# A four-layer block on one Trainium2 core: the later part of a woven feed-forward placed one head later, and the context copies of the next batch placed in other heads

## The chip, the core and the metric

The kernel runs on one core of one Trainium2 chip. The metric is the device time of one execution in microseconds (us), the median of several. The kernel before takes 576.02 us (median of three runs, 575.34 to 576.35).

## The reference

Four residual steps act on `x` (4 batches, 256 tokens, 256 columns): a selective state-space scan over a context, a mixture of 64 experts (8 per token), a cross-attention with 16 heads, and a feed-forward with weights rounded to -1, 0, 1. Each is added under a tanh gate. Only the last two matter here.

```python
x = x + tanh(g_xattn[0]) * L0_xattn(ctx_1024, layernorm(x), ...)
x = x + tanh(g_ffn[0])   * L0_ffn(layernorm(x), ...)          # experts
x = x + tanh(g_xattn[1]) * L1_xattn(layernorm(x), ctx_1024, ...)
x = x + tanh(g_ffn[1])   * L1_ffn(x, ...)

# L1_xattn, per batch and head (16 heads, 8 key/value heads, width 128)
scores = q @ k.T / sqrt(128); attn = softmax(scores); out = attn @ v; return out @ Wo
# L1_ffn
h = silu(bitlinear158(x, w1, b1))     # rms norm, 8-bit rounding of rows, ternary weights
h = gelu(h)
h = layer_norm(h, ln_g, ln_b)
return bitlinear158(h, w2, b2)        # inner width 1024
```

## The kernel before, in words

Every engine has its own program, written in the order in which it shall run, and waits on counting semaphores. Scan, routing and experts come first. From about 283 us on, the attention of the four batches runs head by head, in 64 turns called slots here: slot s is head s mod 16 of batch s div 16. Key and query weights are folded into one matrix `mqk` per head, value and output weights into `nvo`, so that the keys are the context itself. Products of fp32 accuracy are made of three products of rounded parts: a value is copied as fp32r (`..._high`, on ACT), and its remainder is made beside it (`..._low`, on DVE).

In one slot each engine does this for heads of different age:

- PE turns the weights of head s-3 (`turn_p`, L1617), makes the scores of head s (`cT,qT`, L1567 to L1569), the values of head s-4 (L1628), the query product of head s+2 (`xnT,mqk`) and the output product of head s-5 (`nvo,oT`).
- ACT copies the turned weights of head s-3 (`pT`, L1027), the value product of head s-4 (`oT`, L1033) and the query of head s+2 (`qT`, L1012), and makes the exponentials of head s (`pr`, L1019).
- DVE makes the reciprocal of head s-1 (`pinv`, L2293), masks the scores of head s (L2284), and makes the remainders `oT` and `qT` (L2254).
- POOL normalises head s-1 (`pn`, L688). It waits for the reciprocal; PE's turn and ACT's next exponentials but one wait for it.

Into this the feed-forward of the batch before is woven, for the first three batches. `feeds(slot)` returns for a slot the pairs (f, at): batch f, and `at` = slot - 16 (f + 1), from 0 to 27. The tables in each engine's loop say what a batch does at which `at`. Batches 0 and 1 (f < B - 2) share one table, batch 2 has another. For batches 0 and 1 the back part, from the gelu on, is: `gelu` (13), `rest_rows` (14), `middle`, `deviations` (15, 16), `variance`, `centred` (16), `root_of` with `frt` (POOL, L696), `normal_hidden` (17), `squares`, `largest`, `mean_square` (17, 18), `root_of` with `frm`, `scaled` and `scale_round` (19), `turn_hidden` (20), `turned_hidden`, `out_of` and `finish` (22). The front part of the next batch begins at its own `at` 5, which is `at` 21 of this one: `front_stats` 5, `front_norm` 6, `front_round` 7, `turn_in` 8, `into` 9 and 11. `hidden`, `silu` and `gated` follow at 10 to 13.

Two more things stand between the heads. The next batch's inputs of attention: its context as fp32r (`context_high`, ACT, L993, tile `cT`), the remainder of that (`context_low`, DVE), the context rows (`context_rows`, ACT, L997, tile `cS`), the normalised rows (`norm3`, `turn_xn3`, `norm_high`, `norm_low`, tile `xnT`, in heads 12 and 13). And POOL's `gather` (L672): 16 indirect DMAs fetch the expert rows of batch b + 1 in heads 0 to 7 of batch b, for b = 0, 1, 2. Batch 3 has none.

Of the kernel before, what the change touches and what calls it, by code (L numbers as in the profile page):

```python
# [60 lines left out]
def build_program(nc, t, out):  # L61

    with ExitStack() as ctx:
# [491 lines left out]
        def _(pool):  # L555
# [171 lines left out]
            for slot in range(NH * B + 5):  # L727
# [29 lines left out]
                for f, at in feeds(slot):  # L757
                    if at == 5:
                        root_front(f)
                    if at == (14 if f < B - 2 else 12):  # L760
                        rest_rows(f)
                    if at == (15 if f < B - 2 else 14):
                        root_of(f, 1, 0)
                    if at == (17 if f < B - 2 else 19):
                        root_of(f, 1, 1)
# [10 lines left out]
        def _(act):  # L776
# [344 lines left out]
            for slot in range(NH * B + 5):  # L1121
# [3 lines left out]
                if b + 1 < B:  # L1125
                    if h == 13:
                        context_high(b + 1)
                for f, at in feeds(slot):
                    if at == 9 and f < B - 2:
                        turned(f)  # L1130
                    if at == (12 if f < B - 2 else 10):
                        silu(f, 1)
                    if at == 12 and f == B - 2:
                        gelu(f, 0)
                        gelu(f, 1)
                    if at == 18 and f < B - 2:
                        squares(f, 1)
                    if at == 22 and f < B - 2:
                        turned_hidden(f, 0)
                    if at == (22 if f < B - 2 else 20):  # L1140
                        turned_hidden(f, 1)
# [4 lines left out]
                for f, at in feeds(slot):  # L1146
                    if at == 8 and f == B - 2:
                        turned(f)
                    if at == 13 and f == B - 2:
                        deviations(f, 0)  # L1150
                    if at == 16 and f < B - 2:
                        deviations(f, 1)
                    if at == 16 and f == B - 2:
                        squares(f, 1)
                    if at == 19 and f == B - 2:
                        turned_hidden(f, 0)
# [9 lines left out]
                for f, at in feeds(slot):  # L1166
                    if at == (11 if f < B - 2 else 9):
                        silu(f, 0)
                    if at == 13 and f < B - 2:
                        gelu(f, 0)  # L1170
                        gelu(f, 1)
                    if at == 15 and f < B - 2:
                        deviations(f, 0)
                    if at == 14 and f == B - 2:
                        deviations(f, 1)
                    if at == (17 if f < B - 2 else 15):
                        squares(f, 0)
# [21 lines left out]
        def _(pe):  # L1199
# [536 lines left out]
            for slot in range(NH * B + 9):  # L1736
# [17 lines left out]
                for f, at in feeds(slot):  # L1754
# [6 lines left out]
                    if at == (20 if f < B - 2 else 19):  # L1761
                        turn_hidden(f, 0)
                    if at == (20 if f < B - 2 else 24):
                        turn_hidden(f, 1)
                    if at == (22 if f < B - 2 else 24):
# [20 lines left out]
        def _(dve):  # L1786
# [836 lines left out]
            for slot in range(NH * B + 12):  # L2623
# [8 lines left out]
                if b + 1 < B:  # L2632
# [11 lines left out]
                    if h == 13:  # L2644
                        context_low(b + 1)
                for f, at in feeds(slot):
# [12 lines left out]
                    if at == (16 if f < B - 2 else 14):  # L2659
# [3 lines left out]
                    if at == (17 if f < B - 2 else 15):  # L2663
                        normal_hidden(f, 0)
                    if at == 17 and f < B - 2:
                        normal_hidden(f, 1)
                    if at == (18 if f < B - 2 else 16):
# [3 lines left out]
                    if at == 18 and f < B - 2:  # L2671
                        mean_square(f)
                    if at == (19 if f < B - 2 else 17):
# [19 lines left out]
                for f, at in feeds(slot):  # L2693
# [13 lines left out]
                    if at == (15 if f < B - 2 else 12):  # L2707
                        middle(f)
                    if at == 16 and f < B - 2:
# [4 lines left out]
                    if at == 18 and f < B - 2:  # L2714
# [3 lines left out]
                    if at == (19 if f < B - 2 else 17):  # L2718
                        scale_round(f, 0)
                    if at == 19 and f < B - 2:  # L2720
                        scale_round(f, 1)
                    if at == 22 and f < B - 2:
# [64 lines left out]
```

## Time and profile before

| | before |
|---|---|
| median of 3 runs | 576.02 us |
| profiled execution | 575.79 us |
| its span | 573.8 us |
| mean granted TensorE clock | 0.955 |
| attention, slots 0 to 63 | about 283 to 531 us |
| busy: PE, DVE, ACT, POOL | 84%, 82%, 64%, 49% |

The profile is of one execution, which took 575.79 us; its span from first to last instruction is 573.8 us, so 2.0 us lie around it, and it stands 0.23 us below the median. A matmul row of PE has a modelled end. An idle time in brackets stands before the instruction of its row, with what ended it.

### The profile page before, as it was taken

Reading aid. Unit: us, or ns where it says so; the run is one execution under the profiler, and the core shown is the slowest. Engines: PE = TensorE matmul, PEld = TensorE weight load, DVE = VectorE, ACT = ScalarE, POOL = GpSimd, SP = SyncE. Lnnn points to the kernel's source line nnn. Section 1 sums busy time; section 2 is a strip of 40 time slices with the busy share of each in tenths; the row PEclk is TensorE's granted clock in tenths of the full one; section 3 lists DMA queues with packets and bytes.
Section 4 is the critical chain, followed back from the end, with each engine's and each line's share of the span. In section 5 each row is a group of like instructions: output and inputs, shape, how many; then the busy total and the mean of one; then the engine's idle time right before and its main releaser. Section 6 shows DMA issues by size and latency. Waiting matters only on the chain.

```text
span 573.8 us, 10348 instructions
## 1 busy us (share of the span) xinstructions
PE 481.4 (84%) x3106; PEld 363.5 (63%) x3106; DVE 472.5 (82%) x1249; ACT 364.4 (64%) x831; POOL 279.7 (49%) x263
## 2 busy tenths in 40 slices
PE   6817777757889899999899999998699988998835
PEld 3302222222368766776888999987589888997714
DVE  4899999999997838788567857896899969875887
ACT  2785555435526555787676666679556796689544
POOL 4118777869520555630287368623874243333111
PEclk9956999999999999999899999999999999999876
DMA  5939400001045889893422012400335000000000
GB/s 155 228 84 324 125 0 1 1 1 37 1 136 154 272 256 295 233 306 104 167 58 63 1 38 57 56 2 1 53 57 61 0 2 2 19 2 1 0 20 19
DMA packets 45626, 48.63 MB, mean 85 GB/s; under 512 B 5660, under 2 KB 42118, under 8 KB 45574
## 3 DMA queue, kind: packets, MB, share of 16 engines
q1 hardware_dynamic: 41734, 36.46, 22.7%
q0 software_dynamic: 3840, 11.54, 9.1%
q8 instruction: 25, 0.41, 0.3%
q14 instruction: 27, 0.22, 0.1%
HBM read 41.43 MB, written 6.56 MB: 84 GB/s over the span
## 4 chain that ended last, share of the span: by engine, by line
PE 32%; DVE 23%; issue 22%; POOL 10%; ACT 7%; DMA 3%; SPq 1%; DVEq 1%; POOLq 0%; ACTq 0%
DVE hst L1884 7%; PE ps L1628 5%; PE ps L1567 3%; PE ps L1568 3%; PE ps L1569 3%; PE ps L1617 2%; POOL G L672 2%; POOL dbu L586 2%; POOL pn L688 2%; PE ps L1277 2%; PE ps L1485 2%; DVE hc L1893 2%; DMA G<-token_rows,idx_x 1%; POOL G L650 1%; PE ps L1521 1%
## 5 line engine op out<-in xcount | busy, mean ns | idle before, releaser
L688 POOL TENSOR_TENSOR pn<-pr,pinv 128x512 f32<-128x512 f32 x64 | 67.6, 1058 | 88.3 <-DVE pinv L2293 87.8
L586 POOL TENSOR_TENSOR dbu<-du,brow 128x512 f32<-128x512 f32 x64 | 81.3, 1282 | 41.6 <-DVE du L1877 23.1
L1277 PE MATMUL ps<-hc,ident 128*128 128x512 f32 x128 | 72.8, 657 | 27.2 <-DVE hc L1893 25.7
L1884 DVE TENSOR_TENSOR_SCAN hst<-ps,dbu 128x512 f32<-128x512 f32 x64 | 77.9, 1217 | 0.2 <-POOL dbu L586 0.2
L831 ACT ACTIVATE ps<-dtv,amat 128x510 f32<-128x510 f32 x64 | 44.1, 690 | 49.1 <-DVE hst L1884 48.2
L1019 ACT ACTIVATE pr<-ebuf,smin 128x256 f32<-128x256 f32 x128 | 63.7, 502 | 13.5 <-POOL pn L688 6.7
L1628 PE MATMUL ps<-pT,cS 128*128 128x256 f32 x256 | 66.5, 382 | 0.0
L1277 PEld LDWEIGHTS ps<-hc,ident 128*128 128x128 f32 x128 | 20.3, 195 | 66.9 <-DVE hc L1893 63.7
L650 POOL DMA_INDIRECT G<-token_rows,idx_x x32 | 37.7, 1179 | 44.2 <-DVE wkv L2019 20.8
L672 POOL DMA_INDIRECT G<-expert_out,idx_g x48 | 51.2, 1066 | 11.6 <-issue 10.7
L2284 DVE CUSTOM_DVE_ANT_0 ebuf<-ps,mbias 128x256 f32<-128x256 f32 x128 | 49.0, 420 | 5.9 <-issue 5.8
L1567 PE MATMUL ps<-xnT,mqk 128*128 128x256 f32 x128 | 46.9, 366 | 6.7 <-DVE qT L2254 3.5
L1617 PE MATMUL ps<-ident,pn 128*128 128x128 f32 x256 | 39.2, 276 | 9.0 <-POOL pn L688 5.1
L1628 PEld LDWEIGHTS ps<-pT,cS 128*128 128x128 f32 x256 | 44.3, 191 | 3.7
L1033 ACT ACTIVATE oT<-ps 128x256 fp32r<-128x256 f32 x64 | 24.4, 381 | 32.5 <-PE ps L1628 31.0
L1567 PE MATMUL ps<-cT,qT 128*128 128x256 f32 x128 | 41.8, 326 | 0.7 <-DVE smin L2284 0.6
L1893 DVE TENSOR_TENSOR hc<-hst,ps 128x512 f32<-128x512 f32 x64 | 42.3, 662 | 0.0
L1027 ACT ACTIVATE pT<-ps 128x512 f32<-128x512 f32 x64 | 37.3, 582 | 4.6 <-PE ps L1617 4.6
L1567 PE MATMUL ps<-nvo,oT 128*128 128x256 f32 x128 | 37.3, 292 | 2.5 <-DVE oT L2254 2.5
L2254 DVE TENSOR_TENSOR oT<-ps,oT 128x256 fp32r<-128x256 f32 x64 | 26.8, 419 | 14.0 <-ACT oT L1033 13.6
L1012 ACT ACTIVATE qT<-ps 128x256 fp32r<-128x256 f32 x64 | 24.6, 384 | 19.7 <-PE ps L1569 18.0
L1617 PEld LDWEIGHTS ps<-ident,pn 128*128 128x128 f32 x256 | 28.9, 141 | 12.6 <-POOL pn L688 6.5
(380 smaller groups left out, 1384.3 us busy)
## 6 DMA issues: line engine op xcount, KB each, us to landing
wdn<-in_L_ffn_wd SPq DMA_DIRECT2D x12, 384.0 KB
wgu<-in_L_ffn_wg SPq DMA_DIRECT2D x11, 384.0 KB
wgu<-in_L_ffn_wu SPq DMA_DIRECT2D x11, 384.0 KB
expert_out<-xn SPq DMA_DIRECT2D x11, 256.0 KB
wq<-in_L_xattn_Wq SPq DMA_DIRECT2D x2, 1024.0 KB, 9.3
wo<-in_L_xattn_Wo SPq DMA_DIRECT2D x1, 2048.0 KB, 15.8
wo<-in_L_ffn_w SPq DMA_DIRECT2D x2, 1024.0 KB, 7.0
expert_out<-pexp SPq DMA_DIRECT2D x5, 256.0 KB
```

The costliest lines, as they stand in the source:

```text
L586: nc.gpsimd.tensor_tensor(dbu[:, j, :], du[:, j % 2, 512 * hb:512 * hb + 512], brow[:, j // 2, :], ALU.mult).then_inc(pool_dbu, 1)
L672: nc.gpsimd.indirect_dma_start(G[:, cc, k, :], None, eout, bass.IndirectOffsetOnAxis(ap=idx_g[:, col:col + 1], axis=0), bounds_check=SLOTS ...
L688: nc.gpsimd.tensor_tensor(pn[:, h % 2], pr[:, h % 2], pinv[:, h % 2, :].unsqueeze(2).to_broadcast([P, 2, L]), ALU.mult)\
L831: A(bank(d).rearrange("p (b l) -> p b l", b=2)[:, :, 1:], dtv[:, d, 512 * hb:512 * hb + 512].rearrange("p (b l) -> p b l", b=2)[:, :, 1:], ...
L1019: last = A(pr[:, h % 2, tt, :], sneg[:, h % 2, tt, :], ACT.Exp, scale=-1.0, bias=smin[:, h % 2, tt:tt + 1], accum_out=psum_[:, h % 2, tt:t ...
L1277: pe.matmul(bank(2 + j % 2), ident[:], hc[:, j % 2, :], start=(isinstance(m, int) and m + k == 0), stop=(isinstance(m, int) and m + k == N ...
L1567: pe.matmul(o, lhs[0], rhs[0], start=start, stop=False)
L1617: last = pe.transpose(ps[:, 4, L * st + P * tt:L * st + P * tt + P], pn[:, h % 2, tt, P * st:P * st + P], ident[:])
L1628: last = pe.matmul(ps[:, 3 + 2 * (h % 2), 0:L], cS[:, b % 2, st, :], pT[:, h % 2, st, :], start=(st == 0), stop=(st == 1))
L1884: V.tensor_tensor_scan(hst[:, j, :], bank(j % 2), dbu[:, j, :], 0.0, ALU.mult, ALU.add)\
L1893: V.tensor_tensor(hc[:, j % 2, :], hst[:, j, :], bank(6 + j // 2), ALU.mult).then_inc(hc_ready, 1)
L2284: last = V.tensor_tensor_reduce(sneg[:, h % 2, tt, :], ps[:, 1, L * tt:L * tt + L], mbias[:, b, :], -(DH ** -0.5), 3e38, ALU.add, ALU.min, ...
```

## The change

The back part of batches 0 and 1 stands one slot later, from the gelu on, on all four engines: `at` 13 becomes 14, and so on up to 23 for `turned_hidden`, `out_of` and `finish`. Batch 2's table and all front parts stay. `context_high` of the next batch moves from head 13 to head 8, for three batches, and `context_low` from head 13 to head 14. No instruction is added or removed. SP's queue is the same.

```diff
--- before.py
+++ after.py
@@ -757,11 +757,11 @@
                 for f, at in feeds(slot):
                     if at == 5:
                         root_front(f)
-                    if at == (14 if f < B - 2 else 12):
+                    if at == (15 if f < B - 2 else 12):
                         rest_rows(f)
-                    if at == (15 if f < B - 2 else 14):
+                    if at == (16 if f < B - 2 else 14):
                         root_of(f, 1, 0)
-                    if at == (17 if f < B - 2 else 19):
+                    if at == (18 if f < B - 2 else 19):
                         root_of(f, 1, 1)
             tail_root_front(0)
             tail_root_front(1)
@@ -1123,7 +1123,7 @@
                 if 3 <= slot < NH * B + 3:
                     turned_p((slot - 3) // NH, (slot - 3) % NH)
                 if b + 1 < B:
-                    if h == 13:
+                    if h == 8:
                         context_high(b + 1)
                 for f, at in feeds(slot):
                     if at == 9 and f < B - 2:
@@ -1133,11 +1133,11 @@
                     if at == 12 and f == B - 2:
                         gelu(f, 0)
                         gelu(f, 1)
-                    if at == 18 and f < B - 2:
+                    if at == 19 and f < B - 2:
                         squares(f, 1)
-                    if at == 22 and f < B - 2:
+                    if at == 23 and f < B - 2:
                         turned_hidden(f, 0)
-                    if at == (22 if f < B - 2 else 20):
+                    if at == (23 if f < B - 2 else 20):
                         turned_hidden(f, 1)
                 if 4 <= slot < NH * B + 4:
                     o_high((slot - 4) // NH, (slot - 4) % NH)
@@ -1148,7 +1148,7 @@
                         turned(f)
                     if at == 13 and f == B - 2:
                         deviations(f, 0)
-                    if at == 16 and f < B - 2:
+                    if at == 17 and f < B - 2:
                         deviations(f, 1)
                     if at == 16 and f == B - 2:
                         squares(f, 1)
@@ -1166,14 +1166,14 @@
                 for f, at in feeds(slot):
                     if at == (11 if f < B - 2 else 9):
                         silu(f, 0)
-                    if at == 13 and f < B - 2:
+                    if at == 14 and f < B - 2:
                         gelu(f, 0)
                         gelu(f, 1)
-                    if at == 15 and f < B - 2:
+                    if at == 16 and f < B - 2:
                         deviations(f, 0)
                     if at == 14 and f == B - 2:
                         deviations(f, 1)
-                    if at == (17 if f < B - 2 else 15):
+                    if at == (18 if f < B - 2 else 15):
                         squares(f, 0)
             tail_turned(0)
             tail_tanh(0, 0)
@@ -1758,11 +1758,11 @@
                         into(f, 0)
                     if at == (11 if f < B - 2 else 9):
                         into(f, 1)
-                    if at == (20 if f < B - 2 else 19):
+                    if at == (21 if f < B - 2 else 19):
                         turn_hidden(f, 0)
-                    if at == (20 if f < B - 2 else 24):
+                    if at == (21 if f < B - 2 else 24):
                         turn_hidden(f, 1)
-                    if at == (22 if f < B - 2 else 24):
+                    if at == (23 if f < B - 2 else 24):
                         out_of(f)
             pe.wait_ge(s_masked, NH * B)
             keep_busy(1, 8)
@@ -2641,7 +2641,7 @@
                         add_experts(b + 1, 0)
                     if h == 12:
                         add_experts(b + 1, 1)
-                    if h == 13:
+                    if h == 14:
                         context_low(b + 1)
                 for f, at in feeds(slot):
                     if at == 5 and f < B - 2:
@@ -2656,21 +2656,21 @@
                         gated(f, 1)
                     if at == 15 and f == B - 2:
                         variance(f)
-                    if at == (16 if f < B - 2 else 14):
+                    if at == (17 if f < B - 2 else 14):
                         centred(f, 0)
                     if at == 15 and f == B - 2:
                         centred(f, 1)
-                    if at == (17 if f < B - 2 else 15):
+                    if at == (18 if f < B - 2 else 15):
                         normal_hidden(f, 0)
-                    if at == 17 and f < B - 2:
+                    if at == 18 and f < B - 2:
                         normal_hidden(f, 1)
-                    if at == (18 if f < B - 2 else 16):
+                    if at == (19 if f < B - 2 else 16):
                         largest(f, 0)
                     if at == 17 and f == B - 2:
                         largest(f, 1)
-                    if at == 18 and f < B - 2:
+                    if at == 19 and f < B - 2:
                         mean_square(f)
-                    if at == (19 if f < B - 2 else 17):
+                    if at == (20 if f < B - 2 else 17):
                         scaled(f)
                     if at == 19 and f == B - 2:
                         scale_round(f, 1)
@@ -2704,22 +2704,22 @@
                         hidden(f, 0)
                     if at == (11 if f < B - 2 else 9):
                         hidden(f, 1)
-                    if at == (15 if f < B - 2 else 12):
+                    if at == (16 if f < B - 2 else 12):
                         middle(f)
-                    if at == 16 and f < B - 2:
+                    if at == 17 and f < B - 2:
                         variance(f)
                         centred(f, 1)
                     if at == 15 and f == B - 2:
                         normal_hidden(f, 1)
-                    if at == 18 and f < B - 2:
+                    if at == 19 and f < B - 2:
                         largest(f, 1)
                     if at == 16 and f == B - 2:
                         mean_square(f)
-                    if at == (19 if f < B - 2 else 17):
+                    if at == (20 if f < B - 2 else 17):
                         scale_round(f, 0)
-                    if at == 19 and f < B - 2:
+                    if at == 20 and f < B - 2:
                         scale_round(f, 1)
-                    if at == 22 and f < B - 2:
+                    if at == 23 and f < B - 2:
                         finish(f)
             tail_add(0)
             tail_stats(0)
```

Three places show what it moves. ACT in heads 13 to 15 of batch 1, before (pT, oT, qT, pr are the copies and exponentials of the slots, xnT_0 the fp32r copy of the normalised rows, L1053 the gelu):

```order
L993 ACTIVATE cT<-ctxT 128x256
L1033 ACTIVATE oT<-ps 128x256
L1012 ACTIVATE qT<-ps 128x256
L1019 ACTIVATE pr,psum_<-ebuf,smin 128x256 x2
L1006 ACTIVATE xnT_0<-ps 128x512
L1053 ACT_TABLE_LOAD
L1053 ACTIVATE wgu,fsum<-wgu 128x1024 x2
L1027 ACTIVATE pT<-ps 128x512
L1033 ACTIVATE oT<-ps 128x256
L1012 ACTIVATE qT<-ps 128x256
L1019 ACT_TABLE_LOAD
```

and in the changed kernel, from the same oT copy on:

```order
L1033 ACTIVATE oT<-ps 128x256
L1012 ACTIVATE qT<-ps 128x256
L1019 ACTIVATE pr,psum_<-ebuf,smin 128x256 x2
L1006 ACTIVATE xnT_0<-ps 128x512
L1027 ACTIVATE pT<-ps 128x512
L1033 ACTIVATE oT<-ps 128x256
L1012 ACTIVATE qT<-ps 128x256
L1019 ACTIVATE pr,psum_<-ebuf,smin 128x256 x2
L997 ACTIVATE cS<-ctx_tm,alive 128x256
L1053 ACT_TABLE_LOAD
L1053 ACTIVATE wgu,fsum<-wgu 128x1024 x2
L1027 ACTIVATE pT<-ps 128x512
```

The gelus have moved behind one whole slot of copies and exponentials and behind the context rows; the context copy `cT` is gone from here.

POOL at the end of batch 1 and in heads 0 and 1 of batch 2 (`pn` is the normalising of a head, `frt` and `frm` the roots of the feed-forward, the `DMA` rows the gathers):

```order
-L688 TENSOR_TENSOR pn<-pr,pinv 128x512
-L696 TENSOR_TENSOR frt<-fve,mhalf 128x2
 L688 TENSOR_TENSOR pn<-pr,pinv 128x512
 L670 TENSOR_TENSOR spare_pool<-mhalf 128x2
 L672 DMA G<-expert_out,idx_g 128x256 x3
+L696 TENSOR_TENSOR frt<-fve,mhalf 128x2
 L688 TENSOR_TENSOR pn<-pr,pinv 128x512
 L672 DMA G<-expert_out,idx_g 128x256 x2
-L696 TENSOR_TENSOR frm<-fms,mhalf 128x2
 L688 TENSOR_TENSOR pn<-pr,pinv 128x512
 L672 DMA G<-expert_out,idx_g 128x256
+L696 TENSOR_TENSOR frm<-fms,mhalf 128x2
```

The root `frt` stood ahead of the first three gathers and the normalising before them; it now stands behind them. `frm` has moved past one normalising and one gather.

DVE in heads 3 to 5 of batch 2 (L2442 and L2445 are `scale_round`, L2304 adds a batch's attention to `x`):

```order
 L2442 TENSOR_SCALAR wgu<-wgu,fqs 128x1024
 L2445 TENSOR_SCALAR wdn<-wgu 128x1024
-L2293 RECIPROCAL pinv<-psum_ 128x2
-L2205 MEMSET spare 128x1
-L2284 ISA ebuf,smin<-ps,mbias 128x256
-L2284 ISA smin 128x1
-L2284 ISA ebuf,smin<-ps,mbias 128x256
-L2284 ISA smin 128x1
-L2254 TENSOR_TENSOR oT<-ps,oT 128x256
-L2254 TENSOR_TENSOR qT<-ps,qT 128x256
 L2304 SCALAR_TENSOR_TENSOR x<-ps,tg,x 128x512
 L2293 RECIPROCAL pinv<-psum_ 128x2
```

A slot of attention work that stood between the rounding and the addition to `x` has gone from between them: they now follow each other.

## Rows read from the trace of the kernel before

**Rows 1.** Busy time, share of the span and instructions of each engine.

```profile
PE 481.4 (84%) x3106; PEld 363.5 (63%) x3106; DVE 472.5 (82%) x1249; ACT 364.4 (64%) x831; POOL 279.7 (49%) x263
```

**Rows 2.** Engines by stretch: slots 19 to 22, 28 to 39, 44 to 55.

```profile
core 0: us, PE busy (x) PEld busy (x) DVE busy (x) ACT busy (x) POOL busy (x), PEclk, DMA share, GB/s
344.71:358.41 13.70, 13.70 (x107) 13.27 (x106) 10.09 (x44) 9.34 (x31) 11.45 (x13) 1.00 0.29 59
377.54:432.49 54.95, 46.56 (x352) 42.56 (x349) 45.44 (x142) 39.39 (x104) 34.16 (x32) 1.00 0.20 32
448.19:498.64 50.45, 45.66 (x351) 42.62 (x350) 42.94 (x141) 39.34 (x104) 18.35 (x17) 1.00 0.02 6
```

**Rows 3.** Timeline of PE (start us, us, instruction, idle before); scores start slots 31, 32, 34, 35, 38.

```profile
388.14 0.39 PE L1567 MATMUL ps<-xnT,mqk 128*128 128x256 f32 x1 [1.20 <-DVE xnT L2254]
...
391.11 0.36 PE L1567 MATMUL ps<-cT,qT 128*128 128x256 f32 x1
...
394.94 0.36 PE L1567 MATMUL ps<-cT,qT 128*128 128x256 f32 x1
...
402.65 0.36 PE L1567 MATMUL ps<-cT,qT 128*128 128x256 f32 x1
...
409.17 0.66 PE L1617 MATMUL ps<-ident,pn 128*128 128x128 f32 x4 [2.32 <-POOL pn L688]
409.58 0.37 PE L1567 MATMUL ps<-cT,qT 128*128 128x256 f32 x1
...
423.87 0.37 PE L1567 MATMUL ps<-cT,qT 128*128 128x256 f32 x1
```

**Rows 4.** Timeline of DVE, slot 29 (head 13 of batch 1).

```profile
384.90 0.79 DVE L2254 TENSOR_TENSOR cT<-ctxT,cT 128x256 fp32r<-128x256 f32 x1
385.61 1.21 DVE L2395 SCALAR_TENSOR_TENSOR wgu<-ebuf,wgu 128x1024 f32<-128x1024 f32 x1
...
387.41 0.68 DVE L2254 TENSOR_TENSOR xnT<-ps,xnT 128x512 fp32r<-128x512 f32 x1
```

**Rows 5.** Timeline of ACT, slots 29 and 30.

```profile
386.61 1.28 ACT L1053 ACT_TABLE_LOAD   x1
...
390.00 0.57 ACT L1027 ACTIVATE pT<-ps 128x512 f32<-128x512 f32 x1
...
391.14 1.28 ACT L1019 ACT_TABLE_LOAD   x1
```

**Rows 6.** Timeline of POOL, slots 31 to 33.

```profile
399.50 1.67 POOL L696 TENSOR_TENSOR frt<-fve,mhalf 128x2 f32<-128x2 f32 x1 [4.65 <-DVE fve L2406]
...
403.48 1.96 POOL L672 DMA_INDIRECT G<-expert_out,idx_g  x1 [0.16 <-issue]
...
408.07 1.05 POOL L688 TENSOR_TENSOR pn<-pr,pinv 128x512 f32<-128x512 f32 x1
```

**Rows 7.** Timeline of DVE, slots 33 and 35.

```profile
401.29 3.17 DVE L2418 SCALAR_TENSOR_TENSOR wgu<-wgu,frt 128x1024 f32<-128x1024 f32 x2
...
412.41 1.00 DVE L2337 TENSOR_TENSOR famax<-famax,frm 128x2 f32<-128x2 f32 x1 [0.80 <-POOL frm L696]
```

**Rows 8.** Timeline of DVE, slots 49 to 53, the same work a batch later.

```profile
471.76 3.95 DVE L2418 SCALAR_TENSOR_TENSOR wgu<-wgu,frt 128x1024 f32<-128x1024 f32 x2
...
480.83 0.51 DVE L2337 TENSOR_TENSOR famax<-famax,frm 128x2 f32<-128x2 f32 x1
...
482.84 0.74 DVE L2442 TENSOR_SCALAR wgu<-wgu,fqs 128x1024 f32<-128x1024 f32 x1
...
485.62 0.16 DVE L2293 RECIPROCAL pinv<-psum_ 128x2 f32<-128x2 f32 x1
...
487.06 0.74 DVE L2304 SCALAR_TENSOR_TENSOR x<-ps,tg,x 128x512 f32<-128x512 f32 x1
```

**Rows 9.** Timeline of PE, the scores of slots 54 and 57.

```profile
490.03 0.37 PE L1567 MATMUL ps<-cT,qT 128*128 128x256 f32 x1
...
502.31 0.37 PE L1567 MATMUL ps<-cT,qT 128*128 128x256 f32 x1
```

## The prediction

> **What bounds the kernel now.** I read the busy line first. PE is busy 84% of the span, DVE 82%, and ACT and POOL have room [rows 1], so neither PE nor DVE can be left alone. I then read the engines by stretch. In slots 19 to 22, with nothing woven in, PE is busy 13.70 of 13.70 us, 3.43 per slot, at full clock; DVE has 10.09 and ACT 9.34 (2.34 per slot) [rows 2]. So an untouched slot is PE's. The two stretches that the change reorders, slots 28 to 39 and 44 to 55, take 54.95 and 50.45 us, with PE busy for 46.56 and 45.66 [rows 2]: 8.4 and 4.8 us of gaps. All that the change can win at once lies there, and nothing in it makes PE's own work shorter. The timeline of PE says what ends the gaps: the remainder of the normalised rows (1.20 us, DVE) and a normalised head that is late (2.32 us, POOL) [rows 3]. So the question is at what time each slot's scores start, before and after. I walk the changed order by hand, with durations of rows of before, on the clock of the old trace; times after are estimates from these.
>
> **First stretch, step 1: heads 13 and 14.** The remainder of `cT` leaves slot 29 and reappears in slot 30. The next DVE instruction starts 0.71 us behind it [rows 4], so the remainder `xnT` starts at 386.70 in place of 387.41 [rows 4]; PE's wait of 1.20 becomes 0.49. In slot 30 the `pT` copy waited until 390.00 behind the table load at 386.61 and both gelus [rows 5]. It now starts at 386.6. So the scores of slot 31 start at about 389.3, not 391.11 [rows 3]: 1.8 us won.
>
> **Step 2: the gelus, a slot later.** The block is not shorter: 3.39 us from its table load to the next copy, plus 1.28 for loading the exponential's table back [rows 5], 4.67 us, where ACT has 3.43 - 2.34 = 1.09 to spare per slot. It now follows the copies, exponentials and context rows of slot 30: query copy at 388.45 (PE's queries end at 388.3), 0.3; exponentials 1.0; context rows 0.4; so 390.15. Plus 3.39 is 393.55; the next `pT` copy takes 0.57 (its row) [rows 5], so PE turns at 394.3 and scores at 394.65, against 394.94 [rows 3]. Of the 1.8 us, 1.5 are given back. **Won so far 0.3.** The exponentials of slot 31 come at 396.0, head 31's reciprocal at 397.1.
>
> **Step 3: POOL.** This is where I look for the gain. Before, `frt` waited 4.65 us for the variance and held back the normalising of head 31 until 401.15; then came three gathers, and head 32 was normalised only from 408.07 to 409.12 [rows 6], which is what PE waited 2.32 us for [rows 3]. Now `frt` stands behind the gathers. Head 31 is normalised at 397.3, the gathers run from 398.6 to 402.6 (about 1.3 each; they are 4 us in which POOL had waited for nothing useful), the variance is ready at 402.6, since the deviations are a slot later too, and `frt` takes 1.67 [rows 6], to 404.5 with its start. Head 32 is done at 405.5 and the scores of slot 35 start at 406.0, against 409.58 [rows 3]. **Won 3.6.** The two gathers of slot 33 now precede the normalising of head 33, done at 409.5, in time.
>
> **Step 4: DVE, slots 34 to 37.** It is the bound from here. Normals from 404.65, 3.1 us for the pair (3.17 in one trace stretch, 3.95 in the other) [rows 7, 8]; remainders of slot 34, 0.67; one masked head 0.77; `largest` twice and remainders, 3.1; mask of slot 36: the scales start at 413.0, against 412.41 one slot earlier [rows 7]. The scales with two remainders took 2.01 in the later batch (480.83 to 482.84) [rows 8], so 1.34 alone; in this batch the first tiny instruction alone took 1.00, not 0.51 [rows 7, 8], and the block ran to 3.4. I take 2.5. Remainders 0.67; the rounding 2.78 (482.84 to 485.62) [rows 8], or 3.0 beside gathers: 419.1. Before, a plain slot of 1.44 us (485.62 to 487.06) [rows 8] followed and let PE run on. Now the addition to `x` (0.66 of its 0.74) [rows 8] and the mask follow at once, and the scores of slot 38 start at 420.65, against 423.87 [rows 3]. **Won 3.2.**
>
> **Step 5: the front part of the next batch.** `finish` now stands in the slot of `front_round`, ahead of it, and needs the output product, which is behind all of PE's slot 39. DVE idles some 1.5 us, finishes (0.9) and rounds (2.1) until 432.5. That is just in time for PE; I charge 0.5 us for the stats one slot after the rounding. **First stretch: 2.7 us won.**
>
> **Second stretch.** Batch 3 has no gathers, so step 3 is absent: head 48 is normalised in step with `frt` before and after. Steps 1 and 2 win 0.3 again. The pair of normals is the slower one, 3.95 [rows 8], and PE waits for the query remainder behind it. Walked the same way, the scales start at 483.9, three microseconds after 480.83 [rows 8], of which a plain slot is only 1.44. Rounding ends at 488.7, the addition and the mask at 490.5, and the scores of slot 54 start at 490.6, against 490.03 [rows 9]: 0.6 lost. The stats, the norm and the late `finish` take 0.4 more: slot 57 at 503.3, against 502.31 [rows 9]. **1.0 us lost.**
>
> **The rest.** `context_high` (0.42 us) in heads 8 lies in ACT's 1.09 us of room; without that cover it would delay one value copy by 0.42. In batch 0 nothing else moves, and PE has no gap in heads 13 and 14 there. `rest_rows` a slot later hides in POOL's waiting. SP and the DMAs it issues are as before; POOL's gathers land earlier than they are used.
>
> **Sum.** -2.7 + 1.0 = -1.7 us. The profiled execution's 575.79 gives 574.1, the median 576.02 gives **574.3**. Bounds: the first stretch wins 0.3 if step 3 fails, and 4.7 if the scales take 1.34 (-1.2) and the late normals cost nothing more (-0.8). The second loses 1.6 if `finish` costs PE its whole 0.6 more, or wins 0.6 if PE keeps step 1. So 570.7 to 577.3.
>
> **A rule against the row.** The normals took 3.17 and 3.95 us for two [rows 7, 8], where a like operation with the same 1,024 columns took 1.21 [rows 4]; the long ones lie beside POOL's normalising and gathers, and one gather beside them took 1.96 [rows 6], others about 1.0. The Trainium skill, page "SBUF — State Buffer", section "Who interferes with whom", says that a VectorE instruction with two SBUF inputs contends with GpSimd's reads but, by inference, not with its descriptor generation. By that rule the gathers would leave the scales of step 4 alone.
>
> **Rivals.**
> - *Nothing held up by gathers.* The scales run in 1.34 us beside them, as in batch 3 [rows 8]. For it: that row. Against it: the gather of 1.96 us [rows 6]. Price -1.2: 573.1, and 572.3 with the 0.8 above. It is what the rule just named would give. Chance 0.18.
> - *The block only moves.* The gelu block costs ACT the same 4.67 us anywhere; if the late exponentials of slot 31 push the variance beyond 404, head 32 is normalised at 407 and step 3 shrinks to about 2, which steps 4 and 5 halve; with the loss of 1.0 the time is 576.0. For it: ACT's idle is nil in slots 30 to 32. Chance 0.24.
> - *Slower: DVE has no plain slot left.* Rounding, addition, stats, norm, `front_round` follow without a gap in slots 36 to 39, and `finish` waits in front. If step 3 wins under 1.3 us, nothing offsets the loss of 1.0 in each stretch: 578.0. For it: DVE is busy 45.44 of 54.95 and 42.94 of 50.45 [rows 2]. Against it: the gathers do leave the path. Chance 0.14.
> - *It doesn't do what it says.* Excluded but for heads 8: the order of the instructions shows the moves.
>
> **The numbers.** The forecast case has 0.44. Under 0.2% (1.15 us) a difference can hardly be told from none, so faster begins at 574.87. Of the forecast case 0.37 lies below it and 0.07 above; with the first rival faster is 0.55. Same: 0.07 and 0.24, 0.31. Slower: 0.14. The range leaves out the tails of the first and third rival: 571.8 to 577.4.
>
> **What would show it.** Right: the scores of slot 31 start some 1.8 us earlier and of slot 32 hardly; `frt` stands behind three gathers with a short wait; PE's gap for a late `pn` falls from 2.32 to about 1; slots 28 to 40 take 2 to 3 us less, slots 44 to 57 about 1 more. Wrong: the gap on `pn` is as long in slot 35 or 36 as before, or the second stretch is shorter too, which would say that PE keeps step 1 and that the front part has room.

## The result: slower by a quarter of a per cent

The change takes 577.28 us (median of 18), the kernel before 576.17 us beside it (median of 18): a ratio of 1.0025, 95% interval 1.0013 to 1.0037. The interval leaves out 1, so the change is slower, though its lower end is under the 0.2% that the prediction took as the least that can be told from none; two further series of the same kernel gave 1.0037 and 1.0027 (below). The forecast was 574.3, faster, with a range of 571.8 to 577.4: the median lies 0.1 us inside the slow end of the range, but on the other side of before. The profiled execution took 575.3 us and was the fastest of its 18; its span is 573.3 us, clock 0.958.

**The profile after.** The busy line of its page:

```profile
PE 477.8 (83%) x3096; PEld 361.6 (63%) x3106; DVE 469.7 (82%) x1249; ACT 365.2 (64%) x831; POOL 279.7 (49%) x263
```

Against [rows 1] PE is busy for 3.6 us less and DVE for 2.8 less, ACT and POOL are within 1 us (10 of PE's rows are missing from this trace): no engine has more to do. In the two stretches below PE is busy for 0.8 us less and 0.1 more than in [rows 2], so what moved there is chiefly its gaps. The same two stretches as in [rows 2], slots 28 to 39 and 44 to 55, by stretch (us; busy us and count of PE, PEld, DVE, ACT, POOL; granted clock; DMA share; GB/s):

```profile
376.66:429.61 52.95, 45.75 (x352) 42.71 (x350) 42.48 (x141) 39.51 (x104) 34.03 (x33) 1.00 0.24 34
445.30:498.11 52.81, 45.72 (x352) 42.68 (x350) 42.07 (x139) 39.56 (x104) 18.39 (x17) 1.00 0.00 1
```

The first takes 52.95 in place of 54.95 us: 2.0 won. The second takes 52.81 in place of 50.45: 2.4 lost. The timeline of PE after, first scores of slots 31, 32, 35, 38, 54 and 57, the turn of head 32 at the start of slot 35, and the output products of head 0 in slots 37 and 53 (start, us, instruction, idle time before it and what ended it):

```profile
388.93 0.36 PE L1567 MATMUL ps<-cT,qT 128*128 128x256 f32 x1
...
394.34 0.37 PE L1567 MATMUL ps<-cT,qT 128*128 128x256 f32 x1
...
405.19 0.66 PE L1617 MATMUL ps<-ident,pn 128*128 128x128 f32 x4 [0.68 <-POOL pn L688]
...
405.60 0.37 PE L1567 MATMUL ps<-cT,qT 128*128 128x256 f32 x1
...
418.95 0.36 PE L1567 MATMUL ps<-nvo,oT 128*128 128x256 f32 x1 [2.96 <-DVE x L2304]
...
421.00 0.36 PE L1567 MATMUL ps<-cT,qT 128*128 128x256 f32 x1
...
487.45 0.35 PE L1567 MATMUL ps<-nvo,oT 128*128 128x256 f32 x1 [2.26 <-DVE x L2304]
...
489.50 0.36 PE L1567 MATMUL ps<-cT,qT 128*128 128x256 f32 x1
...
501.78 0.36 PE L1567 MATMUL ps<-cT,qT 128*128 128x256 f32 x1
```

This execution reached slot 28 at 376.66, the one of before at 377.54 [rows 2]; 0.83 of it had arisen by slot 2, where nothing is edited. Profiles of other kernels reach slot 28 anywhere from 375.74 to 379.68. So from here on every time is a **shift**: how much later than in before the scores of a slot start, counted from the kernel's own slot 28. Slot 31 has 388.93 - 391.11 + 0.88 = -1.3. POOL in the same stretch, against [rows 6]:

```profile
397.05 1.04 POOL L688 TENSOR_TENSOR pn<-pr,pinv 128x512 f32<-128x512 f32 x1 [5.05 <-DVE pinv L2293]
398.40 1.10 POOL L672 DMA_INDIRECT G<-expert_out,idx_g  x1 [0.16 <-issue]
...
402.43 1.69 POOL L696 TENSOR_TENSOR frt<-fve,mhalf 128x2 f32<-128x2 f32 x1 [0.24 <-DVE fve L2406]
404.10 1.03 POOL L688 TENSOR_TENSOR pn<-pr,pinv 128x512 f32<-128x512 f32 x1
```

`frt` stands behind the gathers and its wait has shrunk from 4.65 to 0.24 us; head 32 is normalised at 404.10, not 408.07, each on its own clock. PE's gap of 2.32 us for it [rows 3] has become 0.68. Up to slot 37 nearly all is as intended: its scores start with a shift of -6.1. Then comes a wait that before does not have. DVE in slot 36 and 37 (first tiny instruction of the scales, the roundings, the addition to `x`):

```profile
412.53 0.15 DVE L2337 TENSOR_TENSOR famax<-famax,frm 128x2 f32<-128x2 f32 x1
...
414.19 0.74 DVE L2442 TENSOR_SCALAR wgu<-wgu,fqs 128x1024 f32<-128x1024 f32 x1
414.97 1.77 DVE L2445 TENSOR_SCALAR wdn<-wgu 128x1024 bf16<-128x1024 f32 x1
416.67 0.74 DVE L2442 TENSOR_SCALAR wgu<-wgu,fqs 128x1024 f32<-128x1024 f32 x1
417.44 0.71 DVE L2445 TENSOR_SCALAR wdn<-wgu 128x1024 bf16<-128x1024 f32 x1
418.07 0.73 DVE L2304 SCALAR_TENSOR_TENSOR x<-ps,tg,x 128x512 f32<-128x512 f32 x1
```

and the view of that line's own waits (three executions of it, one per batch; who waited, us in all, times):

```profile
L2304 DVE SCALAR_TENSOR_TENSOR x<-ps,tg,x x3: 730/740/745, 350.6 to 486.6; 128x512 f32<-128x512 f32 x3
...
  PE ps L1567: 5.2, 2
```

PE's `project` waits at head 0 for `x3_ready` (L1638), since the output products of a new batch overwrite the PSUM bank that the addition of the old batch reads. `project` of head 0 stands in slot 5 of a batch, 37 and 53. The addition is DVE's first work of that slot in its own order. Before, the roundings were a slot earlier, and PE waited for them ahead of its slot 37 (timeline of before):

```profile
419.60 0.56 PE L1673 MATMUL ps<-identb,wdn 128*128 128x128 bf16 x7 [0.77 <-DVE wdn L2445]
```

By the time that PE came to its product of slot 37, the addition was done, and nobody waited for it. Now the roundings end right in front of it, PE begins slot 37 some 6 us sooner, and it stands for 2.96 and 2.26 us. The shift falls from -6.1 to -2.0 in slot 38, and from -1.6 in slot 52 to +0.35 in slot 54. At the end of attention (slot 63) it is **+0.35**.

### The profile page after: what moved, and what is told of

Its sections match the earlier page's. It is cut to its first block, busy times and chain, and to the rows that moved or that the text cites. A ratio compares the mean times of both kernels' runs of the same rounds, so it can differ in the third digit from the quotient of the medians.

```text
span 573.3 us, 10338 instructions
## 1 busy us (share of the span) xinstructions
PE 477.8 (83%) x3096; PEld 361.6 (63%) x3106; DVE 469.7 (82%) x1249; ACT 365.2 (64%) x831; POOL 279.7 (49%) x263
## 4 chain that ended last, share of the span: by engine, by line
PE 33%; DVE 23%; issue 21%; POOL 10%; ACT 7%; DMA 3%; SPq 1%; DVEq 1%; POOLq 0%; ACTq 0%; another core or an unknown queue 0%
DVE hst L1884 8%; PE ps L1628 5%; PE ps L1567 4%; PE ps L1568 4%; PE ps L1569 4%; PE ps L1617 3%; POOL dbu L586 3%; DMA G<-token_rows,idx_x 2%; POOL G L672 2%; PE ps L1485 2%; POOL pn L688 2%; POOL G L650 2%; DVE hc L1893 2%; DMA x<-in_x 1%; PE ps L1521 1%
## 5 line engine op out<-in xcount | busy, mean ns | idle before, releaser
L1567 PE MATMUL ps<-nvo,oT 128*128 128x256 f32 x128 | 37.5, 293 | 7.7 <-DVE x L2304 5.2
L1568 PE MATMUL ps<-nvo,oT 128*128 128x256 f32 x128 | 36.0, 281 | 0.0
```

The lines of the kernel that those rows point to most:

```text
L1567: pe.matmul(o, lhs[0], rhs[0], start=start, stop=False)
L1568: pe.matmul(o, lhs[0], rhs[1], start=False, stop=False)
```

## The experiments

All were timed beside runs of the kernel before on the same chip. The median of before differs from series to series (575.73 to 577.16), so only ratios are compared between them. The ratio on record weights the executions otherwise than the quotient of the two medians does, and the two can differ by 0.1% ("first batch only": 0.9945 beside 573.09 / 575.76 = 0.9954). The shifts are of one profiled execution each. That of "first batch only" was the slowest of its six executions, 575.16 us; it reached slot 0 some 2.5 us later than before did, which the shifts leave out.

| kernel | us (runs) | ratio, interval | shift 35 | 38 | 44 | 56 | 63 |
|---|---|---|---|---|---|---|---|
| change | 577.28 (18) | 1.0025 [1.0013, 1.0037] | -3.1 | -2.0 | -2.0 | +0.4 | +0.35 |
| change again | 577.75 (12) | 1.0037 [1.0021, 1.0052] | -3.1 | -1.2 | -0.5 | +1.9 | +1.9 |
| change, third | 577.34 (12) | 1.0027 [1.0014, 1.0040] | -3.1 | -0.7 | -0.4 | +2.0 | +2.0 |
| context alone | 575.82 (12) | 0.9994 [0.9980, 1.0009] | | +0.2 | +0.2 | +0.2 | +0.2 |
| back part alone | 578.16 (12) | 1.0039 [1.0026, 1.0052] | | -1.0 | -0.1 | +2.6 | +2.6 |
| addition early | 573.63 (10) | 0.9958 [0.9945, 0.9971] | -3.1 | -3.2 | -2.8 | -1.3 | -1.3 |
| before, addition early | 576.12 (12) | 0.9995 [0.9977, 1.0013] | | | | | +0.2 |
| first batch only | 573.09 (6) | 0.9945 [0.9924, 0.9966] | -3.1 | -3.2 | -2.8 | -2.6 | -2.55 |
| POOL `frt` alone | 573.86 (11) | 0.9964 [0.9949, 0.9979] | +1.6 | -0.5 | -0.5 | -1.4 | -1.4 |
| POOL both roots | 573.79 (7) | 0.9953 [0.9933, 0.9973] | +1.1 | -1.6 | -1.6 | -2.5 | -2.5 |
| change, PE kept busy | 576.99 (12) | 0.9997 [0.9984, 1.0010] | -3.2 | -2.0 | -2.1 | +0.3 | +0.3 |
| the same again | 576.08 (11) | 1.0014 [0.9998, 1.0029] | -3.1 | -2.0 | -2.0 | +0.35 | +0.35 |
| first batch, POOL for both | 574.09 (8) | 0.9953 [0.9937, 0.9970] | -3.1 | -3.2 | -2.8 | -3.3 | -3.3 |

### Which part: the context moves, or the back part

The kernel before with the two context moves alone (`context_high` in head 8, `context_low` in head 14), and with the back part alone (both copies back in head 13).

> The context copies alone are moved (heads 8 and 14); the back part stays where it was. Theory A (the loss of the change is PE's wait for the addition of a batch's attention to x, 2.96 and 2.26 us in the profile after, because the rounding now stands ahead of it on DVE): that wait is absent here, and ACT's gelus still hold the pT copy until 390.0, so the 0.71 us won on the normalised rows is waited for at the next copy: same as before within 0.5 us. Rival B (the context copies cost the time, for example the ACT copy in head 8 of three batches, 0.42 us each): 0.5 to 1.3 us slower than before.

> The back part alone is one head later; the context copies stay in head 13. Theory A: all of the loss is here, and the remainder of the normalised rows starts 0.71 us later again than in the change, which delays the query copy ahead of the gelus: 1.1 us (the change against before) plus up to 2 x 0.7, so 1.1 to 2.5 us slower than before. Rival B: 0 to 0.6 us slower or even faster than before.

The context moves are worth nothing by themselves (0.9994). The back part alone has the whole loss (1.0039): PE waits 2.97 and 2.25 us for the addition to `x`. Beside it the context moves save a little: the shift at slot 63 is +2.6 without them, and +1.9 and +2.0 in the two profiles of the change with the same slow clock (below).

### The missed wait, taken away

```diff
@@ DVE, start of slot
-                if h == 5 and 0 < b < B:
+                if h == 5 and b == 1:
                     add_attention(b - 1)
@@ DVE, second half of slot, ahead of front_stats
+                if h == 4 and 1 < b < B:
+                    add_attention(b - 1)
```

For batches 1 and 2 the addition stands in slot 36 and 52, ahead of the roundings, once in the change and once in the kernel before.

> The change, and for batches 1 and 2 the addition of attention to x moved on DVE from the start of head 5 to the middle of head 4, ahead of the two roundings. Theory A: PE's wait of 2.96 and 2.26 us for that addition is gone; PE then waits for the roundings instead and wins about 1.25 us in each stretch: 2.5 us faster than the change, about 1.4 us faster than before. Rival C (DVE's queue is simply full in heads 3 to 7, and PE would wait for the mask anyway): within 0.6 us of the change.

> The kernel before, with the same earlier addition for batches 1 and 2 and nothing else. Here the addition stands a plain slot behind the roundings and PE doesn't wait for it. Theory A: same as before within 0.5 us (the addition now waits for the last output product of the batch, which may cost DVE a little). If it is faster by 1 us or more, the earlier addition has a worth of its own, and what the third kernel wins says nothing of the change.

The change with this edit takes 573.63 us, ratio 0.9958, and the shift of slot 38 is -3.2 rather than -2.0. In before the same edit does nothing (0.9995): there nobody waits for the addition. So the wait takes the gain away. It costs 1.2 us of shift at slot 38, of which 0.8 is left at slot 44 (-2.0 against -2.8), and 0.8 in the second stretch (lost from slot 44 to 56: 1.5 rather than 2.4): 1.6 us in all. PE's timeline with the edit, turns of slots 37 and 53:

```profile
416.60 0.62 PE L1673 MATMUL ps<-identb,wdn 128*128 128x128 bf16 x8 [0.84 <-DVE wdn L2445]
...
485.77 0.62 PE L1673 MATMUL ps<-identb,wdn 128*128 128x128 bf16 x8 [0.77 <-DVE wdn L2445]
```

What is late next are the roundings themselves, 0.8 us at a time. The medians gained more than the profiles: 1.0025 - 0.9958 is 0.7% of 576, or 4 us, where the shifts differ by 1.6. So one profile of the change is not enough.

### The change again, twice, and PE kept busy in its wait

The first profile of the change was of its fastest execution of 18. Here the change is run twice more, with nothing edited.

> The change itself a second time, for a second profile: its first profile was of the fastest of 18 executions. Theory A: the same waits of PE for the addition to x, 2.9 and 2.3 us, and an attention 0 to 1.5 us longer than before. If the first stretch differs by over 1 us from the first profile, the meeting of DVE and the gathers differs from run to run, and that is where the median's excess over the first profile comes from.

> The change a third time, on the same chip as the next kernel, for a third profile and a direct comparison. Theory K: its first stretch is either as in the first profile (2.0 us shorter than before, full clock) or as in the second (0.4 us shorter, a half-clock spell behind PE's wait); 1.0025 to 1.004 times before. Rival L: a first stretch of some third length at full clock.

Both profiles lose 1.6 us more than the first one, and both at one place: between slots 37 and 40. Four stretches of the third series around PE's wait, which lasts from 416.39 to 419.37 there, columns as above:

```profile
414.00:418.00 4.00, 2.39 (x17) 2.08 (x16) 3.93 (x6) 1.63 (x5) 3.51 (x4) 1.00 0.41 68
418.00:422.00 4.00, 2.63 (x23) 2.57 (x24) 3.81 (x17) 1.09 (x4) 2.90 (x4) 0.75 0.37 66
422.00:426.00 4.00, 4.00 (x28) 3.90 (x27) 1.94 (x8) 1.40 (x4) 2.34 (x3) 0.82 0.02 4
426.00:430.00 4.00, 4.00 (x34) 3.81 (x33) 2.76 (x12) 4.00 (x10) 3.52 (x4) 1.00 0.44 77
```

and in the change's first profile, the same stretch:

```profile
418.00:422.00 4.00, 3.05 (x33) 3.03 (x34) 3.39 (x17) 1.69 (x5) 3.24 (x4) 1.00 0.54 66
422.00:426.00 4.00, 4.00 (x31) 3.83 (x29) 3.93 (x16) 2.82 (x8) 3.23 (x4) 1.00 0.24 35
```

The granted clock falls from 1.00 to 0.75 and 0.82 of these stretches: for a while it is at the lower of its two levels, 1.2 GHz for 2.4, just after PE's wait of 2.98 us; a matmul takes 0.41 us in place of 0.28. So in three of four profiles with this order (0.93 and 0.64 in the change again, 0.91 and 0.67 with the back part alone) the wait costs a second time. The wait of 2.26 us in slot 53 does not: from 440 to 530 us the granted clock is 1.00 in all four. The Trainium skill, page "TensorE: Matmul & The Clock Gate", section "HAM oscillation — how this bites in real kernels", describes longer waits, for a DMA between groups of matmuls, that let the clock fall, with the next group run at the lower level. These traces agree on the fall and the slow group, for a wait of under 3 us for another engine, and not in every execution. To test whether it is the idleness, PE was given useless transposes just ahead of its wait:

```diff
@@ PE, ahead of project
+                if h == 5 and b in (2, 3):
+                    pe.wait_ge(f_h, 2 * (b - 1))
+                    keep_busy(7, 20)
```

> The change, with 20 transposes of the identity into a free PSUM bank ahead of the output product of head 0, in batches 2 and 3, where PE waits 2.96 and 2.26 us for the addition to x. Their results are not used. They take less than those waits, so they delay nothing that waited. Theory K (in the executions where PE's granted clock falls to half after that wait, as in the second profile of the change, 0.77 in the stretch where the first has 1.00, the first stretch takes 1.55 us more; that is most of what the median has over the first profile): full clock through the first stretch, stretches as in the first profile of the change, median 1 to 1.5 us under the change's, 576.2 to 576.8. Rival L (the half clock has another cause, or the median's excess lies outside the attention): median within 0.5 us of the change, 577.3 to 577.8.

> The change with PE kept busy during the two waits, a second time. Theory K: no half-clock spell between slots 28 and 63, first stretch 2.0 to 2.1 us shorter than before, and 1 to 2 us faster than the change of the same call. Rival L: within 0.5 us of it.

The second was run in the series of the change's third. It takes 576.08 where the change takes 577.34, 1.26 us less, with more work; by the ratios, 1.0014 and 1.0027, it is 0.7 us, and their intervals overlap. Over all series the two kernels with transposes have 0.9997 and 1.0014, the change 1.0025, 1.0037 and 1.0027: 1.4 us between the means. Its stretches and its PE (the transposes, then the product behind its wait):

```profile
414.00:418.00 4.00, 4.00 (x34) 3.89 (x33) 3.92 (x6) 1.90 (x7) 3.51 (x4) 1.00 0.39 59
418.00:422.00 4.00, 3.21 (x36) 2.96 (x35) 3.89 (x18) 1.13 (x5) 2.95 (x4) 1.00 0.45 74
422.00:426.00 4.00, 4.00 (x33) 3.89 (x32) 3.42 (x14) 2.70 (x9) 3.35 (x4) 1.00 0.11 24
```

```profile
416.50 2.35 PE L1283 MATMUL ps<-ident 128*128 128x128 f32 x20
...
419.63 0.36 PE L1567 MATMUL ps<-nvo,oT 128*128 128x256 f32 x1 [0.79 <-DVE x L2307]
```

L2307 is the addition here, since the edit adds three lines above it. The product starts no earlier against slot 28 than in the change, the clock stays at 1.00, and the shift stays at +0.3 and +0.35. So the slower clock costs 1.6 us in a profile that has it and, as a mean over executions, some 1.4. Two profiles without a fall could still be chance, where one in four has none anyway; that the times agree makes it likely, not certain. Of the 4 us between the change and the early addition, the wait has 1.6 and the clock up to 1.6; the rest, some 0.7, is within what the intervals allow and stays open, as does why the clock did not fall in one of the four profiles.

### Only the batch that has gathers beside it

The second stretch has no gathers, so the later back part should only lose there. Every number of the back part that was changed is put back for batch 1, and only the addition of slot 36, for the first stretch, is early (one of the changed lines; the others are alike):

```diff
-                    if at == (16 if f < B - 2 else 14):
+                    if at == (16 - (f == 1) if f < B - 2 else 14):
                         root_of(f, 1, 0)
...
```

> The context copies moved as in the change; the back part one head later for batch 0 alone (first stretch), batch 1's as before; the addition to x early for the first stretch alone. Theory A, with its second half (a later back part pays only where gathers stand in POOL's queue; without them it loses 1.5 us even with the early addition, as the third kernel's second stretch did): attention 2.9 us shorter than before, so 572.9, about 1.5 us faster than the third kernel. Rival D (the gain of the third kernel is spread over both stretches): no faster than the third kernel, 573.6 or more.

573.09 us, 0.9945. The shift is -2.8 at slot 44 and still -2.6 at 56: the second stretch loses 0.3, where it lost 1.5 with the early addition and batch 1's back part late. So the later back part helps batch 0 and harms batch 1.

### POOL's order alone

The kernel before with `frt` of batches 0 and 1 behind the gathers of its slot (`root_of(f, 1, 0)` at 16 for 15), and with `frm` a slot later too (18 for 17):

> The kernel before with one change: on POOL the first root of the back part (frt) is issued one head later, so that it stands behind the normalising of head 31 and the first three gathers, as in the change. PE, ACT and DVE keep their order. Theory P (the gain of the first stretch is this order, since the root's wait of 4.65 us held up the gathers and then head 32): first stretch 2 to 3 us shorter, second 0.3 to 0.6 shorter (PE's 0.64 us wait for head 47 gone): 572.5 to 573.5. Rival Q (the gain came from ACT and DVE in heads 13 and 14, or the root now comes late for the pair of normals): within 0.6 us of before.

> As the kernel with the one root moved, and the second root (frm) one head later too, behind one more normalising and one gather. Theory P: up to 1 us faster again, if the wait of the scales for frm isn't longer by the 2.3 us of these two; if it is, up to 1 us slower than with the one root moved. Rival Q: within 0.6 us of before.

Both gain as a whole (0.9964 and 0.9953), but not where I expected the 2 to 3 us: the first stretch won 0.5 with `frt` alone. The normals are not a slot later here, so DVE waits for `frt`, and PE for the query remainder queued behind them. With `frt` alone, DVE, PE, and a stretch behind PE's gap (columns as above):

```profile
403.20 3.26 DVE L2418 SCALAR_TENSOR_TENSOR wgu<-wgu,frt 128x1024 f32<-128x1024 f32 x2 [2.20 <-POOL frt L696]
```

```profile
407.18 0.58 PE L1567 MATMUL ps<-xnT,mqk 128*128 128x256 f32 x1 [3.95 <-DVE qT L2254]
```

```profile
407.00:411.00 4.00, 3.82 (x18) 3.82 (x19) 3.95 (x13) 2.60 (x8) 2.28 (x3) 0.50 0.35 61
```

Behind this gap of 3.95 us too the clock is at its lower level, a granted 0.50 over the stretch. Slot 35 is 1.6 us late, and the gathers, off the path by then, give 2.0 back by slot 37. In the second stretch POOL's order alone wins 1.0: `frt` no longer stands and waits for the variance ahead of a normalisation, and PE's gap of 0.64 us for head 47 is gone. In the first stretch POOL's two roots alone are worth 1.6, where the whole move with the early addition wins 2.8: there the other engines' move adds 1.2, in the second it takes the gain away. The rest of the move without POOL's roots was not run, so what it would do alone is open.

The two findings together: batch 0 as in the change with the early addition, batch 1 with POOL's two numbers alone.

> The kernel with the later back part and early addition in the first stretch alone (attention 2.55 us shorter than before in its profile), with the two roots on POOL one head later in the second stretch as well, where they alone won 0.95 us. If gains of different stretches add: attention 3.4 to 3.5 us shorter than before, median 572.2 to 572.6. If the second stretch's gain depends on how the first one ends: no better than 573.1.

Its profile has the longest gain in attention, -3.3, but its ratio (0.9953) is no better than that of the first batch only (0.9945); the intervals overlap, so nothing says which is the better kernel. Four versions lie between 0.9945 and 0.9958 and are not to be ranked; all of them beat both kernels.

## Why the prediction was wrong

**Steps 1 and 2 (heads 13 and 14, the gelus): right, 0.5 us too kind.** The scores of slot 31 won 1.3 us (1.8 forecast), those of slot 32 lost 0.28 (0.3 won forecast). ACT after:

```profile
389.85 1.28 ACT L1053 ACT_TABLE_LOAD   x1
...
393.24 0.57 ACT L1027 ACTIVATE pT<-ps 128x512 f32<-128x512 f32 x1
394.38 1.28 ACT L1019 ACT_TABLE_LOAD   x1
```

From table load to next copy the block takes 3.39 us, as in [rows 5]. PE's remaining wait for `xnT` was 0.86, not 0.49.

**Step 3 (POOL): right.** Slot 35 won 3.1 (3.6 forecast; the 0.5 is that of step 2), and head 32 was normalised at 404.10 + 0.88 = 404.98 on the clock of before, 404.5 forecast.

**Step 4 (DVE, slots 34 to 37): this is the step that failed.** DVE's times came out, in part by luck. The scales began at 413.4 (413.0 forecast) and the roundings ended at 418.95 (419.1), both on the clock of before. But the scales took 1.0 us, not 2.5, and the roundings 3.9, not 3.0 (414.19 to 418.07): two sizes were off and nearly cancel. "Now the addition to `x` and the mask follow at once" was right for DVE. But I asked only when DVE would be ready for the scores of slot 38, and let PE run its products of slot 37 in the meantime. The release of PE's product by that addition was not in the sum: by the forecast's own times the addition ended at 419.75, and PE stood at its product from 416.9 (418.95 - 2.96 + 0.88). From that product to the next scores PE has another 2.05 us of work (418.95 to 421.00), the turning of the rounded rows among it: 419.75 + 2.05 = 421.8, where step 4 had 420.65. The measured start is 421.00 + 0.88 = 421.9, so 3.2 won became 2.0. With the early addition it is 3.2 again, as forecast, with PE waiting for the roundings instead: the product's wait is what the step had left out.

**Step 5 (the next front part): right.** From slot 38 to 40 the early addition's kernel loses 0.16, and 0.4 up to slot 44; 0.5 was charged.

**Second stretch: the same omission.** 1.0 us lost was forecast, 2.4 came. Of the difference the wait is 0.8, by the early addition; the other 0.5 is an undersized price of the late back part, and no run here splits it further.

**The sum.** Forecast -2.7 + 1.0. Without the missed wait it is -2.8 + 1.5 = -1.3; the kernel with the early addition is 0.4% or 2.4 us faster than before, 1.1 more than its shift, which stays open. With the wait it is -2.0 + 2.4 = +0.35, which gives 576.5, and with the slower clock, 1.6 more, 578.1; the median of 577.28 lies between. So the missed wait alone, 1.6 us, turned -1.3 into +0.35, and by these numbers it was the clock that made the loss large enough to measure.

**The rivals.** "Slower" came true in sign and was the nearest in time, 578.0. It named the right engine, slots and lack of a plain slot, yet not the wait that decides, and its condition (step 3 wins under 1.3) did not hold. "Nothing held up by gathers" was right in its row: the scales ran from 412.53 to 413.52, 1.0 us, beside gathers. The Trainium skill, page "SBUF — State Buffer", section "Who interferes with whom", would have it so, and for these tiny instructions the trace agrees. For the long ones it is open: a gather that ran beside the pair of normals took 1.89 us (1.96 before [rows 6]), the others of slots 32 to 37 0.99 to 1.32. What had stretched the scales before was not a gather but POOL's normalising. The instruction of 1.00 us at 412.41 [rows 7] ends with the normalising of 412.36 to 413.39, and the last of the block ends with the next one (DVE and POOL, before):

```profile
414.04 1.72 DVE L2344 SCALAR_TENSOR_TENSOR fqs<-fqs,frm 128x2 f32<-128x2 f32 x1
```

```profile
414.68 1.05 POOL L688 TENSOR_TENSOR pn<-pr,pinv 128x512 f32<-128x512 f32 x1
```

After the change a normalising (415.14 to 416.19) met the first rounding instead, which took 1.77 us against 0.71 for the second, and that used up most of what the scales saved. "The block only moves" is excluded by slot 35.

## What to carry to other kernels

When work is moved in one engine's queue, list for every instruction that now stands behind it which semaphore it raises and who waits for that, not only the data that the moved work itself makes: a buffer's release for reuse is as hard an edge as a result. Walk the waiting engine to that edge at its new, earlier time, since a gain ahead of it can be the very thing that makes the wait. And split a move by engine and by batch: here one queue's order held more than half of the gain, and the same edit that helped where gathers compete only cost where they don't.

## What the runs showed of the hardware

- Behind one wait of PE of 2.95 to 2.98 us the granted clock fell to its lower level in three profiles of four (as low as 0.64 over 4 us), which cost 1.6 us more; behind the later wait of 2.26 us it fell in none. In both profiles with 20 transposes, 2.35 us in all, ahead of the wait, the clock stayed at 1.00.
- The first profile of the change had no such drop and lay 2 us below its own median: taken alone it would have made the change look no slower than before (575.3 us against 575.79). Where median and profile differ by that much, a second profile is worth its run.
- A rounding of 1,024 columns (f32 to bf16) beside POOL's normalising took 1.76 to 1.77 us in place of 0.71, longer by the 1.05 us of the normalising, in all four profiles of this order. Beside it two of the tiny scales took 1.00 and 1.72 us in before, in place of 0.15 and 0.16. Beside a gather the scales took 0.16 to 0.27 us each.
